# Last head of an attention kernel: weights made in five places, and who rounds which step

## The reference

```python
x = x + xattn0(layernorm(x), ctx)      # 16 heads of width 16, 896 queries, 16 * 1500 = 24000 keys
x = x + moe0(layernorm(x))             # 32 experts, 6 chosen, and a shared one
x = x + xattn1(layernorm(x), ctx)      # a decaying scan over each context, then its mean
x = x + moe1(layernorm(x))

def xattn0(x, cond):                   # q, k, v rounded to 127 steps a head's row or column
    attn = softmax(q @ k.T)
    attn = round(attn * 255 / max) ... # the weights of a query rounded to 255 steps of their largest
    return (attn @ v) @ Wp + bp

def xattn1(Z, kv):                     # K = sigmoid(decay)
    s_t = K * s_(t-1) + (kv_t @ W_in.T + b_in)
    summary = mean over t of (s_t @ W_out.T + b_out)
    return layernorm(Z + summary) * gamma + beta
```

## Time and profile before

| | |
|---|---|
| three runs, median | 4506.83 us (4506.46 to 4507.93) |
| the profiled execution | 4505.41 us, span 4503.7 us |
| mean granted clock of TensorE | 0.988 |
| busy in the span: TensorE matmuls | 4293.8 us, 95% |
| VectorE | 4020.6 us, 89% |
| GpSimd | 3679.2 us, 82% |
| ScalarE | 3525.6 us, 78% |

### The profile page before, as it was taken

The page is one execution under the profiler, slowest core; times in us unless marked ns, Lnnn a source line. Parts: engine busy times, 40 slices in busy tenths (PEclk is TensorE's granted clock), DMA queues, the critical chain, the costliest instruction groups (busy, mean ns, idle before and its releaser), DMA issues. The chain is left out here.

```text
span 4503.7 us, 134862 instructions
## 1 busy us (share of the span) xinstructions
PE 4293.8 (95%) x54175; PEld 1769.0 (39%) x54175; DVE 4020.6 (89%) x7371; ACT 3525.6 (78%) x3643; POOL 3679.2 (82%) x4026
## 2 busy tenths in 40 slices
PE   7888888999999999999999999999999999888999
PEld 5666663333333333333333333333333333224655
DVE  6888888999999999999999999999999999884333
ACT  3555557899999999999999999999999999882111
POOL 5777777999999999999999999999999999872000
PEclk9999998999999999999999999999999999999999
DMA  3555542111111111111111111111111111442010
GB/s 103 162 165 170 168 151 68 36 36 33 37 35 33 37 35 34 36 34 34 37 33 36 35 34 36 33 36 35 34 36 37 31 38 32 158 147 94 0 39 9
DMA packets 222678, 267.79 MB, mean 59 GB/s; under 512 B 34366, under 2 KB 202809, under 8 KB 221289
## 3 DMA queue, kind: packets, MB, share of 16 engines
q1 hardware_dynamic: 167529, 203.57, 16.1%
q10 hardware_dynamic: 54528, 55.60, 3.9%
HBM read 174.57 MB, written 82.97 MB: 57 GB/s over the span
## 5 line engine op out<-in xcount | busy, mean ns | idle before, releaser
L1580 ACT ACTIVATE e_home<-ps_scores,sk 125x896 f32<-125x896 f32 x3072 | 3076.7, 1009 | 276.8 <-PE ps_scores L1318 68.2
L1614 DVE TENSOR_REDUCE unit_max<-ps_maxima 128x1 f32<-128x428 f32 (+2 forms) x5760 | 3068.7, 607 | 28.1 <-PE ps_maxima L1346 20.1
L1801 POOL TENSOR_SCALAR r<-e_home 125x896 f32<-125x896 f32 x2976 | 2759.0, 956 | 187.6 <-POOLq L104 94.4
L1374 PE MATMUL ps_maxima<-e_home,unit 125*17 125x224 f32 x24576 | 1691.7, 352 | 8.2 <-DVE r L1648 7.2
L1318 PE MATMUL ps_scores<-q,k_home 54*128 54x448 bf16 x5760 | 1585.2, 355 | 3.1 <-PEq L1493 2.9
L1346 PE MATMUL ps_maxima<-k_home,q 48*128 48x428 bf16 (+2 forms) x5760 | 1574.9, 351 | 2.1
L1366 PE MATMUL ps_maxima<-r,vt 125*16 125x224 f16 x12288 | 850.7, 267 | 32.6 <-DVE r L1648 21.0
L1318 PEld LDWEIGHTS ps_scores<-q,k_home 54*128 54x128 bf16 x5760 | 323.5, 95 | 1060.7 <-issue 1045.6
L1366 PEld LDWEIGHTS ps_maxima<-r,vt 125*16 125x16 f16 x12288 | 294.4, 85 | 1060.0 <-issue 831.2
L1374 PEld LDWEIGHTS ps_maxima<-e_home,unit 125*17 125x17 f32 x24576 | 616.8, 95 | 13.8 <-DVE r L1648 7.5
L1346 PEld LDWEIGHTS ps_maxima<-k_home,q 48*128 48x128 bf16 x5760 | 376.6, 93 | 56.4 <-DVE unit_max L1614 44.6
(11 more groups left out here) (272 smaller groups left out, 2738.2 us busy)
## 6 DMA issues: line engine op xcount, KB each, us to landing
k_rows<-krows ACTq DMA_DIRECT2D x48, 1000.0 KB, 6.9
k_home<-k_rows SPq DMA_DIRECT2D x408, 93.8 KB
k_home<-k_rows SPq DMA_DIRECT2D x120, 281.2 KB
e_home<-in_ctxT SPq DMA_DIRECT2D x48, 500.0 KB, 5.4
vr<-v_raw SPq DMA_DIRECT2D x128, 187.5 KB
cb<-in_ctxT SPq DMA_DIRECT2D x16, 1500.0 KB, 6.1
v_raw<-e_home SPq DMA_DIRECT2D x12, 1000.0 KB
v_raw<-vb SPq DMA_DIRECT2D x12, 1000.0 KB
```

Source lines behind the costliest of these rows:

```text
L1374: made = pe.matmul(psav[c:c + WIDE, lo:hi], unit[:, :], e[(i + s) % SLOTS][0:KT, g, lo:hi], start=head_first and part == 0, stop=False, sk ...
L1580: act.activation(e[i % SLOTS][0:KT, :, :], score_banks(i)[0:KT, :, :], ACT.Exp, scale=sk[u][:, i:i + 1]).then_inc(e_wrote[h % 2], 1)
L1614: top = dve.tensor_reduce(maxima[y][:, b, slot:slot + 1], ps[:, 0:hi - lo], axis=AX.X, op=ALU.max)
L1801: pool.tensor_scalar(r[i % SLOTS][:, :, :], e[i % SLOTS][0:KT, :, :], 1.0, WHOLE_WORD, ALU.mult, ALU.add)\
```

## The change

The row of weights is no longer made in one go before the first chunk of the last head: `weights(part)` makes one instruction in each of the steps 0, 2, 4, 8 and 10 of that chunk, behind VectorE's rounding of the step where there is one. The four context sums of this chunk move from steps 0, 4, 8, 12 to 12, 15, 18, 22; those of the other chunks stay. A function `by_vector(j, i)` says which steps VectorE rounds: in chunks 1 to 4 the odd ones, as before; in chunks 0, 5, 6 and 7 only the steps 1, 5, 9, 13, 17, 21. The others are GpSimd's, whose list takes them in, and TensorE's `sums` waits for a pair accordingly: for one of each semaphore where VectorE has the odd step, for two of `r_ready` where it hasn't.

```diff
@@ -1075,6 +1075,12 @@
     MAIN = STEPS - len(EARLY)
     SCALED, WHOLE, CHAINED = (1, 4), (SLOTS - 1, SLOTS + 2), 13
     WEIGHED = (0, 4, 8, 12)
+    WEIGHTS, WEIGHED_FIRST = (0, 2, 4, 8, 10), (12, 15, 18, 22)
+
+    def by_vector(j, i):
+
+        return i % 2 == 1 and (0 < j < NCH - 3 or i % 4 == 1)
+
 
     def attention():
         st = ExitStack()
@@ -1467,9 +1473,10 @@
             def head(h1, h2, finished, y, more):
                 first, second = h1 is not None, h2 is not None
 
-                def step_sums(i, u, head_start):
+                def step_sums(j, i, u, head_start):
 
                     at = i - LAG - i % 2
+                    shared = not first and by_vector(*divmod(j * CT + at + 1, CT))
                     if not second or head_start and i == LAG:
                         return
                     if head_start and at == 0:
@@ -1477,13 +1484,13 @@
                             sums_read()
                         else:
                             clear_sums()
-                        sums(0, u, 0, shared=not first, head_first=True)
-                        sums(0, u, 1, shared=not first, head_first=True)
+                        sums(0, u, 0, shared=shared, head_first=True)
+                        sums(0, u, 1, shared=shared, head_first=True)
                     elif at >= 0:
-                        sums(at, u, i % 2, shared=not first)
+                        sums(at, u, i % 2, shared=shared)
                     elif not head_start or finished is not None:
                         sums(at + CT, 1 - u, i % 2, head_end=head_start and i == LAG - 1,
-                             shared=not first and not head_start)
+                             shared=shared and not head_start)
 
                 def chunk(j, u, head_start, last):
                     if second and head_start:
@@ -1505,7 +1512,7 @@
                             turn_scales()
                         if (j, i) in SPREAD:
                             spread_z(*SPREAD[j, i])
-                        step_sums(i, u, head_start)
+                        step_sums(j, i, u, head_start)
                     for i in range(CT) if first else ():
                         todo = pieces(j * CT + i, finished is not None, more)
                         if second and (i >= 2 or not head_start or finished is not None):
@@ -1542,22 +1549,22 @@
                     last = pe.matmul(ps1[0][:, m * BATCH:(m + 1) * BATCH], w_in[:, c, m * P:(m + 1) * P], ctx_sum[:, c, :],
                                      start=(c == 0), stop=(c == NC - 1))
             last.then_inc(x_sum_ready, 1)
-            sums(CT - 6, 1, 0, shared=True)
+            sums(CT - 6, 1, 0, shared=by_vector(NCH - 1, CT - 5))
             last_exponentials(CT - 2)
-            sums(CT - 6, 1, 1, shared=True)
+            sums(CT - 6, 1, 1, shared=by_vector(NCH - 1, CT - 5))
             last_exponentials(CT - 1)
             pe.wait_ge(heads_ready, 1).then_inc(heads_ready, -1)
             pe.wait_ge(wp_ready, 1).then_inc(wp_ready, -1)
-            sums(CT - 4, 1, 0, shared=True)
+            sums(CT - 4, 1, 0, shared=by_vector(NCH - 1, CT - 3))
             pe.wait_ge(mean_ready, 1).then_inc(mean_ready, -1)
             for c in range(NC):
                 last = pe.matmul(ps1[1][0:BATCH, 0:DIM], mean[:, c, :], w_out[:, c, :],
                                  start=(c == 0), stop=(c == NC - 1))
             last.then_inc(proj_ready, 1)
             project((4, 5))
-            sums(CT - 4, 1, 1, shared=True)
-            sums(CT - 2, 1, 0, shared=True)
-            sums(CT - 2, 1, 1, shared=True, final=True)
+            sums(CT - 4, 1, 1, shared=by_vector(NCH - 1, CT - 3))
+            sums(CT - 2, 1, 0, shared=by_vector(NCH - 1, CT - 1))
+            sums(CT - 2, 1, 1, shared=by_vector(NCH - 1, CT - 1), final=True)
             even.clear()
             odd.clear()
             project_last()
@@ -1635,12 +1642,17 @@
                     dve.sem_inc(s1_free, 1)
                     dve.sem_inc(q2_ready, 1)
 
-            def weights():
-                dve_done(dve.memset(ones_c[:, :], 1.0))
-                dve_done(dve.tensor_scalar(keep[:, :], ones_c[:, :], decay[:, 0:1], None, ALU.mult))
-                dve_done(dve.tensor_tensor_scan(weight[:, :], keep[:, :], ones_c[:, :], 0.0, ALU.mult, ALU.add))
-                dve_done(dve.tensor_reduce(wsum[:, :], weight[:, :], axis=AX.X, op=ALU.add))
-                dve_done(dve.tensor_copy(keep[:, :], weight[:, ::-1]))
+            def weights(part):
+                if part == 0:
+                    dve_done(dve.memset(ones_c[:, :], 1.0))
+                if part == 1:
+                    dve_done(dve.tensor_scalar(keep[:, :], ones_c[:, :], decay[:, 0:1], None, ALU.mult))
+                if part == 2:
+                    dve_done(dve.tensor_tensor_scan(weight[:, :], keep[:, :], ones_c[:, :], 0.0, ALU.mult, ALU.add))
+                if part == 3:
+                    dve_done(dve.tensor_reduce(wsum[:, :], weight[:, :], axis=AX.X, op=ALU.add))
+                if part == 4:
+                    dve_done(dve.tensor_copy(keep[:, :], weight[:, ::-1]))
 
             def rounded(j, i):
 
@@ -1734,16 +1746,17 @@
                 first, second = h1 is not None, h2 is not None
 
                 def chunk(j, u, head_start, last):
-                    if not first and head_start:
-                        weights()
+                    weighed = WEIGHED_FIRST if head_start else WEIGHED
                     made.settle()
                     for i in range(CT):
                         step = j * CT + i
                         todo = pieces(step, finished is not None, more) if first else []
-                        if not first and i % 2 == 1:
+                        if not first and by_vector(j, i):
                             rounded(j, i)
-                        if not first and i in WEIGHED:
-                            weigh_context(j * 2 + WEIGHED.index(i) // NC, WEIGHED.index(i) % NC)
+                        if not first and head_start and i in WEIGHTS:
+                            weights(WEIGHTS.index(i))
+                        if not first and i in weighed:
+                            weigh_context(j * 2 + weighed.index(i) // NC, weighed.index(i) % NC)
                         if not first:
                             kept_sums(j, i)
                         if first and step == MAIN:
@@ -1804,7 +1817,7 @@
             def chunk(n, u, h, shared):
 
                 for i in range(CT):
-                    if not shared or i % 2 == 0:
+                    if not shared or not by_vector(n % NCH, i):
                         rounded(n, i)
                     if n % NCH == NCH - 1 and i == CHAINED and n // NCH < HEADS - 1:
                         turn_shift(n // NCH + 1)
```

## The result

The changed kernel takes 4513.41 us (median of 20 runs, 4511.59 to 4515.46); the kernel before, run beside it, 4506.53 (20 runs). The ratio is 1.0015, with a 95% interval of 1.0008 to 1.0021: slower by some 7 us, 0.15%. The forecast was 4506.0 within 4499 to 4513, so the measured time lies just outside the range, on the slow side. The profiled execution took 4512.1 us (span 4510.1; before 4505.41 and 4503.7): 6.4 us more in the span.

The account below looks back on a forecast made before the run. TensorE and ScalarE set each chunk's floor; VectorE and GpSimd block each other. Terms -1.4 +4.0 -3.1 -1.5 -1.3 = -3.3, with the layout's shortfall -1.5, with the tail -0.8: profiled 4504.6, median 4506.0, range 4499 to 4513.

Parts of the forecast that it names:

- The wait of 7.2 us: Chunk 0, kernel before: TensorE waits for VectorE's rounding of step 1, behind the weights' instructions; forecast to go.
- The layout by instruction: VectorE's and GpSimd's lists timed one instruction after another; chunk 0 30.1 us, chunks 2 to 4 with six roundings moved 27.3.
- the ledger alone: Sum of times VectorE and GpSimd hold something both need in turn; 0.32 us more per moved rounding, 24.8 for chunks 2 to 4.
- Rival A: GpSimd keeps up, chunk 1 stays 23.9, chunks 5 to 7 give 5.9: -13, 4494 us; chance 0.08.
- the paragraph on chunk 1: Chunk 1: GpSimd starts late and stands up to 2.5 us for late values; 27.9 us, 4.0 more, ends 23.9 and 31.
- the steps at the low clock: Chunk 0: TensorE's steps at the low clock add 1.3 us to its 30.1.
- the middle: Chunk 5: 26.9 us, between the ledger's 25.7 and GpSimd's list at 28.0; 3.1 less than before.
- the upper end, 28.0: GpSimd's list in chunk 5 if every turn falls badly; taken for chunk 6, 1.5 less than before.
- The tail: After chunk 7's last score: GpSimd ends its roundings some 2 us later; pair 18 is used at once, 0.7 more.
- the 1.8 added back: The same layout of the order before came out 1.8 us short of the trace, so the sum went from -3.3 to -1.5.
- B: GpSimd becomes the bound in chunks 5 to 7 too, values late; chunk 0 +1, chunk 1 +6: +10, 4517 us; chance 0.05.
- the 0.2% that had 0.88: Chance 0.88 that the run changes by no more than 0.2%, about 9 us; faster 0.07, slower 0.05.

Follow-up runs that it names:

- the fifth experiment: Kernel before, with only the values that GpSimd takes in chunk 1 issued later, behind the keys: 4510.05 us, ratio 1.0008.
- The third experiment: Changed kernel, with the next chunk's values issued between the two contexts instead of behind both (chunks 1 to 6 of the last head): 4507.17 us, ratio 1.0002.

## Why the prediction was wrong

**Right.** The wait of 7.2 us went, and GpSimd took over as the late one: waits of 2.5, 0.8 and 2.9 us for 3.6 and 2.8, in their places. GpSimd's longest rounding in chunk 0 was 3.68 us for some 4. The layout by instruction gave 27.3 us for a chunk with six roundings moved, and 27.2 were measured; that is one number, the ledger alone had 24.8, and 2.5 us of it are low clock. The late second context, the values behind it and GpSimd standing in chunk 1 were seen, chunks 3 and 4 stayed, chunk 7 gave 1.4 for 1.3. GpSimd asked for the values at 3889.1, where 3889.5 was laid out. Rival A, the gain without a successor, fell by chunk 0's length.

**Wrong.** The step that failed is the values' landing in the paragraph on chunk 1: "a context needs 6.1 us to land", "the values come behind it, near 3892", "up to 2.5 us of standing". The order was right and the size was not: they were taken at 3895.87, 10.1 us after their issue, and GpSimd stood 6.75 us. A context load right ahead of the values is not new: before it went out 0.5 us ahead of them too, and the forecast counted it. What is new is that the keys of chunk 2 go out 0.4 us behind the values and no longer 7. The prediction says of the keys that "moving them costs nothing"; it asks only when they are due, and not what they do to a load that is still under way.

The DMA packets in the traces show how the 10.1 us divide. A load of values is 375 packets of 512 bytes. With no context close ahead (the fifth experiment) the last of them ends 3.5 us after the issue. With a context right ahead and no keys near it is 6.8 in the kernel before; over all traces 44 of 46 such loads (no keys within 6.5 us) have 6.4 to 7.0, the other two 9.0 and 10.2 for a reason not shown. With the context ahead and the keys right behind it is 9.0 in the changed kernel, and 8.3 to 9.9 in eight such loads over three traces. So the context ahead makes some 3.3 us and the keys some 2.1; GpSimd begins 0.6 to 1.1 after the last packet. Without the keys the values would have come near 3893.5 by these figures (an estimate): the forecast also allowed too little for the values' own time behind the context.

**What this step is worth.** The third experiment, which takes the standing away, is 6.2 us faster by the medians, and that alone would have brought the time into the range. That its 4507.17 lies 1.2 us from the forecast of 4506.0 is luck in part. Its chunk 0 is 2.8 us above the term of the sum, chunks 5 and 6 are 2.2 and 1.5 above theirs, and chunk 1 is 1.1 below. Its trace also shows less than the medians: chunk 1 is 2.3 us shorter than in the changed kernel, chunk 2 1.5 and the whole span 2.7, since the profiled execution (4509.46) is one of the slowest of its ten.

**The other terms, which don't cancel.** In the profiled execution the sum missed by 7.2 us: -0.8 was forecast, +6.4 measured. Chunk 1, where the standing is, has 1.3 of that, since the layout had 4.7 us of waiting there already, for 6.25 measured. Chunk 0 has the largest part, 2.7. Its waits were right (6.2 us for 6.4); the steps at the low clock were sized at 1.3 us, and TensorE's matmuls are busy 25.7 us there for 21.4 at the full clock, 4.3 more.

```profile
3851.64:3884.44 32.80, 25.66 (x344) 8.48 (x344) 22.43 (x19) 23.21 (x27) 30.11 (x25) 0.84 0.21 69
```

In the run with the values first chunk 0 is still 32.9, so this has nothing to do with the values. Chunk 2, priced at nothing, has 1.5: its own old waits of 0.7 and 1.6 us are followed there by steps at the low clock, as in several of the experiments, while before no chunk from 1 to 4 had any. Chunks 5 and 6 gave 1.0 and 0 for 3.1 and 1.5: "the middle" between ledger and GpSimd's list was too kind for chunk 5, and at 29.1 and 29.5 both chunks lie above even the upper end, 28.0; in chunk 5 TensorE waits 5.3 us for roundings of GpSimd's. The tail took 1.3 for 0.7; the runs with the rounding of step 23 moved have 440.4 to 441.1 there against 439.6 to 439.7 in three without, though others without it have 440.7 to 442.4, so the cause of this 1 us is not shown. Against all these stood the 1.8 added back, a start 0.6 earlier, and 0.1 in chunk 7.

**The rivals.** B, given 0.05, came nearer than the forecast: 4517 against 4506.0 for 4513.4. It named the right places for the loss, with +1 for chunk 0 against 1.3 measured, +6 for chunk 1 against 5.3, and late values among its parts, but chunks 5 to 7 got shorter and not longer, and it had the wrong condition: it was to decide by GpSimd's hold of 0.84 us. The DMA decided. The change of 0.15% lies within the 0.2% that had 0.88; the range, at 0.87, was 0.4 us too short on the slow side.

## What to carry to other kernels

When work is moved later, follow the buffers that it frees through the queue that refills them: what stands behind that load in an in-order queue comes later too, even if it has nothing to do with the moved work. Put loads that an engine waits for ahead of those that wait for a buffer; here that one order made 6 us in one kernel and 28 in another. Then look at what is issued right behind it as well: the keys lengthened the values' transfer by some 2 us. And price such a load by all that is issued around it, not by its own landing.

## What the runs showed of the hardware

The same load of 187.5 KB could be used 4.1 us after its issue with no context load close ahead of it, and 10.1 us after it when it stood between a context of 1500 KB and the keys. Its last packet ended 3.5 us after the issue with neither near, 6.8 with the context ahead, and 9.0 with the context ahead and the keys behind.

VectorE's and GpSimd's roundings lengthen each other: VectorE's takes 0.63 us by itself and GpSimd's 0.94, and where they alternate VectorE's four take 4.29. The split of 18 to 6 instead of 12 to 12 made chunks 3.3 us longer with the same number of roundings, 2.5 of them at the low clock.

The low level of TensorE's clock (1.2 GHz) came back after the waits of 0.7 and 1.6 us in some runs (chunk 2 at 25.3 to 25.4 us) and not in others (23.9) with the same work and the same waits; in the kernel before it did so in none of chunks 1 to 4. Why in one and not in another isn't settled by these runs; it moves single executions by some 1.5 us for each such chunk.
